# Four heads' reciprocal sums: one narrow transposition and two transfers through DRAM in place of four wide transpositions

## The reference

```
scores = einsum('bnhd,bmhd->bhnm', q, k) * scale      # 8 heads, 512 x 512
attn   = softmax(where(adj == 0, -inf, scores), axis=-1)
h      = einsum('bhnm,bmhd->bnhd', attn, v).reshape(b, n, d)
y      = h @ Wo + bo + x ;  out = layer_norm(y) * gamma + beta
```

## Time and profile before

| | us |
|---|---|
| median of 3 runs | 1202.79 (1202.02 to 1202.92) |
| the profiled execution, its own time | 1202.1 |
| its span, first to last instruction | 1200.0 |
| PE busy | 1154.6 (96%) |
| DVE busy | 982.9 (82%) |
| ACT busy | 928.5 (77%) |
| POOL busy | 530.9 (44%) |

### The profile page before, as it was taken

The page is one execution under the profiler, slowest core; times in us unless marked ns, Lnnn a source line. Parts: engine busy times, 40 slices in busy tenths (PEclk is TensorE's granted clock), DMA queues, the critical chain, the costliest instruction groups (busy, mean ns, idle before and its releaser), DMA issues.

```text
span 1200.0 us, 28462 instructions
## 1 busy us (share of the span) xinstructions
PE 1154.6 (96%) x9596; PEld 843.5 (70%) x9596; DVE 982.9 (82%) x2688; ACT 928.5 (77%) x2115; POOL 530.9 (44%) x398
## 2 busy tenths in 40 slices
PE   7788999999999999999999999999999999999796
PEld 4566677777777777777777777777777777777463
DVE  5777788888888888888888888888888888988776
ACT  4426887888888788888878888887888888788774
POOL 1222445443564444356444534644453464444330
PEclk9898999999999999999999999999999999999999
DMA  8015160532517053251615325261432516122311
GB/s 228 19 36 141 20 190 24 148 81 73 140 37 194 19 141 90 72 141 36 180 33 136 89 72 148 36 179 34 127 89 80 148 36 180 34 71 72 111 32 36
DMA packets 164446, 112.48 MB, mean 94 GB/s; under 512 B 100944, under 2 KB 146000, under 8 KB 164304
## 3 DMA queue, kind: packets, MB, share of 16 engines
q1 hardware_dynamic: 162144, 102.80, 33.1%
q0 software_dynamic: 2160, 7.87, 1.9%
HBM read 61.87 MB, written 25.17 MB: 73 GB/s over the span
## 4 chain that ended last, share of the span: by engine, by line
PE 87%; DVE 6%; issue 2%; ACT 2%; DMA 2%; POOL 1%; DVEq 0%; SPq 0%; POOLq 0%; ACTq 0%
PE ps_j L848 39%; PE ps_t L861 22%; PE ps_j L988 9%; PE ps_s L840 8%; PE ps_s L834 6%; ACT probs L1048 1%; DMA xt<-ys 1%; DVE masked_s L1149 1%; PE ps_j L996 1%; POOL ys L674 1%; PE ps_j L955 0%; DVE wq L1199 0%; DVE y_l L1268 0%; DMA x<-x_dram 0%; DVE stats_L L1169 0%
## 5 line engine op out<-in xcount | busy, mean ns | idle before, releaser
L1149 DVE CUSTOM_DVE_ANT_0 masked_s<-ps_s,mask 128x512 f32<-128x512 f32 x640 | 424.6, 681 | 21.8 <-PE ps_s L840 20.7
L1048 ACT ACTIVATE probs<-masked_s,nm_h 128x512 f32<-128x512 f32 x512 | 367.3, 718 | 70.4 <-DVE nm_h L1149 63.9
L861 PE MATMUL ps_t<-ident,probs 128*128 128x128 f32 x2560 | 391.3, 276 | 5.6 <-ACT pt_h L1054 2.8
L861 PEld LDWEIGHTS ps_t<-ident,probs 128*128 128x128 f32 x2560 | 306.1, 142 | 85.5 <-issue 23.5
L1054 ACT ACTIVATE pt_h<-ps_t 128x512 f32<-128x512 f32 x401 | 236.2, 589 | 79.0 <-PE ps_t L861 74.3
L840 PE MATMUL ps_s<-stack 128*128 128x512 f16 x512 | 194.5, 380 | 2.6 <-DVE nm_h L1149 1.7
L848 PE MATMUL ps_j<-xw,pt_l 128*128 128x256 f16 x1536 | 189.1, 274 | 2.1 <-DVE xw L1294 2.1
L848 PEld LDWEIGHTS ps_j<-xw,pt_l 128*128 128x128 f16 x1536 | 151.0, 98 | 32.9 <-issue 2.2
L656 POOL TENSOR_TENSOR rstd_L<-var_eps_L,minus_half 128x4 f32<-128x4 f32 x32 | 32.8, 1024 | 246.5 <-DVE var_eps_L L1179 246.5
L988 PE MATMUL ps_j<-pt_h,v 128*32 128x256 f32 x2048 | 123.6, 382 | 2.4 <-DVE pt_h L1156 2.4
L1184 DVE TENSOR_TENSOR pt_l<-ps_t,pt_l 128x512 f16<-128x512 f32 x128 | 88.3, 690 | 32.5 <-ACT pt_l L1054 26.1
(11 more groups left out here) (140 smaller groups left out, 1639.4 us busy)
## 6 DMA issues: line engine op xcount, KB each, us to landing
stack<-bounce SPq DMA_DIRECT2D x256, 128.0 KB, 3.1
bounce<-parts SPq DMA_DIRECT2D x64, 256.0 KB, 2.6
adj_t<-adj_dram SPq DMA_DIRECT2D x30, 512.0 KB, 5.2
x<-x_dram SPq DMA_DIRECT2D x16, 512.0 KB, 3.9
out_dram<-y_f POOLq DMA_DIRECT2D x15, 512.0 KB, 3.4
stack<-adj_dram SPq DMA_DIRECT2D x2, 512.0 KB, 5.6
pt_h<-l_wc SPq DMA_DIRECT2D x2, 256.0 KB, 4.6
out_dram<-y_f SPq DMA_DIRECT2D x4, 128.0 KB, 1.8
```

Of the source, the lines that this page charges most:

```text
L861: last = pe.transpose(ps_t[r % 2][:, t], probs[:, r, t * P:(t + 1) * P], ident[:])
L1048: act.activation(probs[:, r], masked_s[:, r], ACT.Exp, bias=nm[:, n, r:r + 1], scale=-1.0, accum_out=total[:, n, r:r + 1]).then_inc(exps, 1)
L1149: dve.tensor_tensor_reduce(out=masked_s[:, r], in0=ps_s[scores_bank(pos)][:], in1=m[:, r], scale=-scale, scalar=NONE_LEFT, op0=ALU.add, op ...
```

## The change

For graphs 0 to 13, all that the loop handles (`spread_by_dma`), the reciprocals take another way; the last two graphs, in the tail, keep the old one.

- New job `RT` with two parts, at steps 5 and 7 (group 0) and 25 and 27 (group 1). Part 0: PE transposes r_h as it is, 128 x 16 to 16 x 128, in one instruction. ACT copies the 16 rows of 128 to r_rows and issues their transfer to the DRAM tensor `spread`. Part 1: ACT waits until that has landed and issues a transfer from `spread` to rb, in which each of the four heads' 512 values goes to 32 partitions.
- ACT's widening of r_h, PE's four transpositions and ACT's copy of them to rb are left out for these graphs.
- `OG` part 2 is DVE's multiplication alone. It waits for the second transfer, and stands at steps 10 and 29 in place of 7 and 26.
- The banks of XW of layer 1 change from (1, 0) to (0, 1), those of WO from (0, 2) to (2, 0). Their steps stay.

```diff
-    ("OG", (1, 0), "i", 0, (3, 5, 7)),
+    ("RT", (0, 0), "i", 0, (5, 7)),
+    ("OG", (1, 0), "i", 0, (3, 5, 10)),
...
-    ("OG", (1, 2), "i", 1, (22, 24, 26)),
+    ("RT", (2, 2), "i", 1, (25, 27)),
+    ("OG", (1, 2), "i", 1, (22, 24, 29)),
...
-    ("XW", (1, 0), "i+2", 1, (30, 35)),
-    ("WO", (0, 2), "i", 0, (32, 34)),
+    ("XW", (0, 1), "i+2", 1, (30, 35)),
+    ("WO", (2, 0), "i", 0, (32, 34)),
...
+        r_rows = sb("r_rows", [4 * NT, P])
+        spread = nc.dram_tensor("spread", [4 * NT, P], fp32).ap()
...
+        def spread_by_dma(b):
+            return b < LOOPS
+        def rb_spread(b, g):
+            if spread_by_dma(b):
+                return rb_in, 16 * (2 * b + g + 1)
+            return rb_ready, FIRST + 2 * (b - LOOPS) + g + 1
...  PE, bank():
-                        pe.wait_ge(rb_ready if half else ot_ready, FIRST + 2 * b + l + 1)
+                        pe.wait_ge(*rb_spread(b, l) if half else (ot_ready, FIRST + 2 * b + l + 1))
+                    if name == "RT":
+                        pe.wait_ge(r_rows_ready, 2 * b + l + 1)
...  PE, job():
+                if name == "RT" and half == 0:
+                    pe.wait_ge(r_h_ready, 2 * b + l + 1)
+                    out_bank = bank(banks[0], before)
+                    pe.transpose(out_bank[0:4 * NT, 0:P], r_h[:].rearrange("p h t -> p (h t)"), ident[:])\
+                        .then_inc(done["RB"], 1)
...
-                    else:
-                        pe.wait_ge(r_wide_ready, 2 * b + g + 1)
+                    elif not spread_by_dma(b):
+                        pe.wait_ge(r_wide_ready, 2 * (b - LOOPS) + g + 1)
...  ACT, job():
-                if name == "R":
+                if name == "R" and not spread_by_dma(b):
...
-                if name == "OG" and half == 2:
+                if name == "RT" and half == 0:
+                    G = 2 * b + l
+                    act.wait_ge(done["RB"], FIRST + G + 1)
+                    if G > 0:
+                        act.wait_ge(r_rows_out, 16 * G)
+                        act.wait_ge(rb_in, 16 * G)
+                    act.activation(r_rows[:], bank[0:4 * NT, 0:P], ACT.Copy).then_inc(r_rows_ready, 1)
+                    act.wait_ge(r_rows_ready, G + 1)
+                    act.dma_start(spread, r_rows[:]).then_inc(r_rows_out, 16)
+                if name == "RT" and half == 1:
+                    G = 2 * b + l
+                    act.wait_ge(r_rows_out, 16 * (G + 1))
+                    act.wait_ge(ot_ready, FIRST + G)
+                    act.dma_start(rb[:], spread.rearrange("(h t) q -> h (t q)", t=NT).unsqueeze(1)
+                                  .to_broadcast([4, HD, N])).then_inc(rb_in, 16)
+                if name == "OG" and half == 2 and not spread_by_dma(b):
...  DVE, job():
-                    dve.wait_ge(rb_ready, FIRST + 2 * b + g + 1)
+                    dve.wait_ge(*rb_spread(b, g))
```

More of the change, by code:

```diff
@@ L262, in graph_attention @@
         rb_ready, ot_ready = sem("rb_ready"), sem("ot_ready")
+        r_rows_ready, r_rows_out, rb_in = sem("r_rows_ready"), sem("r_rows_out"), sem("rb_in")
         ot_hi, ot_lo = sem("ot_hi"), sem("ot_lo")
@@ L449, in occupy @@
                     return before
+                if half == (2 if name == "OG" and spread_by_dma(b) else 1 if name == "RT" else None):
+                    return ()
                 side = half // 2 if name in ("AV", "OG") else half
@@ L1260, in job @@
                     make_mask(b, l)
-                if name in "SDBCZUWM":
+                if name in "SDBCZUWM" or name == "RT":
                     return
```

## The result

The changed kernel takes 1329.6 us (median of 4, 1322.8 to 1335.8) against 1202.4 for the kernel before; the ratio is 1.106 (95% interval 1.104 to 1.108). The direction was forecast, the size was not: 1223 was predicted, with 1237 as the upper end. What was lost is 127 us, 9 us per loop body, where 1.5 had been worked out.

What follows compares the result with a forecast made beforehand. PE was taken to bound the loop, without any wait. Per body a 1.86 us wait at WO less 0.33 us spared gives 1.53, times 14 is 21.4; on 1202.1 that makes 1223 us, range 1210 to 1237.

Steps and rivals of the forecast that it cites:

- What bounds the kernel: Loop bodies: PE is busy for all 70.25 us, so its issued work plus any wait sets the time.
- PE's saving: PE, each group: four transpositions (0.44 us) go, one of 0.11 comes; 0.33 us less, 9.2 us in all.
- ACT: ACT, second group: 0.82 us become free, 1.14 are filled by PE's transposition, copy, signal and issues.
- The net delay of 0.3 us: ACT, second group: qt and what follows, up to kt, start 0.3 us later.
- The moved multiplication: DVE, second group: 5.38 us later against 3.82 us of cover, so PE waits at WO for POOL's ot split.
- the 1.86 of the sum: PE at WO, per body: 1.56 us from the moved multiplication plus 0.3 from ACT's delay of kt.
- 1.56: PE at WO: us by which the ot pair is too late from the moved multiplication, without ACT's delay.
- The two transfers: ACT's write and read of reciprocals: write lands before its wait, read before DVE wants it; no wait.
- Hidden up to 4.0 us: Second group's read: issued about 595.5, wanted by DVE about 599.5, so no wait if landing takes under 4.0 us.
- rival B: Read lands late, 4.8 us after issue, behind DVE's need: 2.08 us per body, 1231 us; chance 0.12.
- The first group: Its later multiplication and its read, wanted some 5 us after issue, are hidden; PE's 0.33 us are kept.
- Masks with room: DVE at 599 to 608: masks run three tiles ahead; PE's wait at WO gives them 1.86 us of room.

Runs made afterwards that it cites:

- experiment 2: Kernel before with only DVE's multiplication moved to steps 10 and 29 and the change's banks, old arithmetic, no transfers: 1228.5 us, ratio 1.022.
- experiment 5: Changed kernel with each head's row four times in DRAM, so one read goes to sixteen engines: 1274.9 us, ratio 1.060.
- experiment 4: Changed kernel with WO at steps 34 and 36 in place of 32 and 34: 1325.6 us, ratio 1.102.
- experiment 3: Kernel before plus both transfers on ACT, constant as source, read on four engines into an unused tile: 1215.0 us, ratio 1.010.
- experiment 7: Changed kernel with 40 products on constants on PE ahead of the wait for ot_h in WO's first part: 1318.4 us, ratio 1.099.
- experiment 6: Kernel without transfers and with DVE's multiplication moved, WO at steps 33 and 34 instead of 32 and 34: 1222.8 us, ratio 1.017.
- experiments 3 and 9: 9: kernel before plus both transfers unused, now 64 rows written and the read on sixteen engines: 1204.8 us, ratio 1.0021.

## Why the prediction was right or wrong

- *What bounds the kernel*: right. PE had no slack, and each stall of PE is in the time.
- *PE's saving*: right in size as far as it can be read, 0.11 us for the narrow transposition. From 644.14 to the next group at 644.25 on PE's timeline are 0.11 us, so going from 128*128 to 128*16 and back cost nothing. (The rule of the Trainium skill, TensorEngine Tiling (Array Packing), Key Properties, on a drain at a change of mode does not show at this place; it did behind 128*32, where the transpositions take 0.59 in the trace before and 0.59 or 0.60 in this one, for 0.44.) The saving is nearly invisible next to the rest.
- *ACT*: right within 0.2 us in each term, 0.25 for the copy, 0.31 and 0.53 for the issues at 0.34. The net delay of 0.3 us does not show: qt starts at 648.23 - 53.00 = 595.23, 0.1 us ahead of its 595.30. (The 2.0 us allowed for the write were not the least of the trace before: its 128 KB stores on SP land after 1.8 in the median. Nothing hung on it.)
- *The moved multiplication*: right in mechanism and nearly in size. Alone it costs 1.87 us per body (experiment 2). That this equals the 1.86 of the sum is luck: the 1.86 held 0.3 for ACT's issues, which experiment 2 does not have. The term to compare is 1.56: experiment 2 has waits of 1.4, and the changed kernel 1.45 as the order's part of its wait. But in the changed kernel it was no longer the term that counts.
- *The two transfers*: this is the step that failed. "Hidden up to 4.0 us" and "hidden as well" rested on the nearest rows, 2.4, 3.1 and 4.8 us for stack<-bounce. Those are transfers whose outer axis is 32 long. The read's is 4, it runs on 3.7 engines, and it took 7.1 and 7.4 us. In the body shown it could be hidden for 4.45 us and came 3.03 us after that; with the order's 1.45 us this is PE's wait at WO, 4.55 us, and over all bodies 4.8 in place of 1.86. It was rival B's mechanism, but B's price went by the same 4.8 and got 1231, within a range that ended at 1237. The rows taken were transfers of 128 KB on sixteen engines, for a read of 256 KB on four: neither the size nor the shape was compared.
- *The first group*: wrong for the same reason, and for two more. Of its 7.1 us, 3.5 pass before the first packet starts and that part is not the number of engines alone: it is 2.7 us on sixteen (experiment 5) and 1.3 in experiment 4, on four. What the read waits for there was not tried apart. And QH's first part takes the bank that the multiplication frees, at step 12, two steps behind. That wait was in the code and missing in the working. Alone it is 0.2 us (experiment 2), with the late read 1.84.
- *What else the transfers delay*: missed. The read held xt<-ys; 12.7 us without any wait for rb (experiment 3).
- *The clock*: missed. With waits of 1.4 us at WO it stayed (experiment 2: mean 0.988); with 3.4 to 6.4 us it fell to 1.2 GHz behind them (mean 0.959), and in experiment 5, where 11 of the 14 waits are 1.6 to 3.3 us, it fell too (0.971). By the estimates above it cost 19 us or more (experiment 7) and up to 41.
- *Masks with room*: right with WO in its place, wrong without: when WO is moved, the same 0.6 us on DVE are PE's wait (experiment 6).

How the 127 us split: 26 are the order. The rest, 101, came only with the transfers: waits for the read, the clock behind them, what the read delays, less the 9.2 us spared. Of these 55 went when the read got 16 engines. The other 46 are, against experiment 2: 25.6 us more at WO and at the first group's bank (43.1 + 4.8 against 19.9 + 2.4), some 22 from the clock (74 us at the lower level against 29, half of the difference), 7.9 in which PE waits for DVE's qt behind ACT, and 9.2 spared.

Of the 43.1 us at WO, 18.9 are three bodies with 6.6, 5.6 and 6.6 us. The packet records of these three second-group reads settle what was late: their first packet starts after 1.8 to 2.3 us, hardly later than in the others (1.4 to 1.9), but the 128 packets then take 5.9 to 6.6 us where the other eleven take 2.0 to 3.3. So the worst cases are made after the first packet has started, not before. What holds the packets up in three bodies of fourteen stays open.

## What to carry to other kernels

Before a transfer is put into a schedule, look at the outer axis of both of its sides and not at its bytes alone: here 4 against 16 was 3.7 against 12.3 engines, and 55 us. A wait on an engine that works in order is paid by everything behind it, so moving the one consumer that shows in the trace (WO) only moved the loss. And when the multiplication of a group is moved, every user of what it frees or feeds has to be looked up, at each engine: the second split on POOL was found that way, the bank of QH was not.

## What the runs showed of the hardware

A broadcast read on four engines hurt the transposing transfer of another queue that ran beside it (landing after 7.7 us in the median instead of 4.5, 12.7 us of the kernel's time) more than the same bytes on sixteen did (5.8 us, 2.7 us; experiments 3 and 9). A write of 8 KB to DRAM landed in 1.5 us in the median of the changed kernel, one of 32 KB in 1.8 (experiment 5). An issue on ACT took 0.31 us for the write of 16 rows, 0.48 for 64, and 0.53 for the read of 128.
